# An inverted-bottleneck convolution on one core: expansion of 8x8 patches without their borders, borders copied inside SBUF

## The reference

```python
def _L0_conv_ref(x, ...):                 # 48 channels, windows of 8x8, 4 heads
    h = windows(layernorm(x))
    q, k, v = qkv(h); attn = softmax(q @ k.T * hd**-0.5 + bias[rel_idx])
    xf = shortcut + proj(attn @ v)
    return xf + fc2(gelu(fc1(layernorm(xf))))

def _L1_conv_ref(x, w1, ..., wd, ..., w2, ...):      # 48 -> 288 -> 48 channels
    h = jnp.einsum('oc,bchw->bohw', w1, x)
    h = jax.nn.relu(_bn(h, g1, b1, m1, v1))
    h = conv_general_dilated(h, wd, padding=((1, 1), (1, 1)), feature_group_count=HID)   # 3x3, depthwise
    h = jax.nn.relu(_bn(h, gd, bd, md, vd))
    h = jnp.einsum('oc,bchw->bohw', w2, h)
    return x + _bn(h, g2, b2, m2, v2)
```

## Time and profile before

| | |
|---|---|
| median of 3 runs | 1952.91 us (1952.12 to 1954.72) |
| span of the profiled execution | 1952.0 us |
| TensorE busy (PE / PEld) | 1870.2 us, 96% / 1565.2 us, 80% |
| VectorE busy | 1445.8 us, 74% |
| ScalarE busy | 1322.8 us, 68% |
| GpSimd busy | 647.1 us, 33% |
| HBM read and written | 128.36 and 54.72 MB, 94 GB/s over the span |
| mean granted TensorE clock | 0.993 of full speed |

### The profile page before, as it was taken

The page is one execution under the profiler, slowest core; times in us unless marked ns, Lnnn a source line. Parts: engine busy times, 40 slices in busy tenths (PEclk is TensorE's granted clock), DMA queues, the critical chain, the costliest instruction groups (busy, mean ns, idle before and its releaser), DMA issues.

```text
span 1952.0 us, 74705 instructions
## 1 busy us (share of the span) xinstructions
PE 1870.2 (96%) x29960; PEld 1565.2 (80%) x29960; DVE 1445.8 (74%) x2650; ACT 1322.8 (68%) x2838; POOL 647.1 (33%) x869
## 2 busy tenths in 40 slices
PE   5999999999999996999999999999999999999998
PEld 4888888888888885555555899999999999999997
DVE  5999999999999997666667556566566566566564
ACT  2788878878888885555555666666666666666665
POOL 4333333333333333413100434325334343344240
PEclk9999999999999998999999999999999999999999
DMA  2222222222222222777664444545363454445331
GB/s 67 68 73 76 78 73 76 77 73 76 77 72 77 74 76 77 182 171 179 161 150 111 97 108 126 99 113 126 87 147 86 112 137 102 103 129 105 99 111 34
DMA packets 286410, 198.43 MB, mean 102 GB/s; under 512 B 225991, under 2 KB 275672, under 8 KB 276504
## 3 DMA queue, kind: packets, MB, share of 16 engines
q1 hardware_dynamic: 282114, 189.12, 37.9%
q0 software_dynamic: 2368, 6.25, 1.5%
q10 hardware_dynamic: 1750, 0.39, 0.1%
HBM read 128.36 MB, written 54.72 MB: 94 GB/s over the span
## 4 chain that ended last, share of the span: by engine, by line
PE 56%; ACT 2%; DMA 1%; issue 1%; DVE 0%; SPq 0%; ACTq 0%; DVEq 0%
PE psum L1126 14%; PE psum L1145 13%; PE psum L1171 9%; PE psum L1180 5%; PE psum L680 5%; PE psum L661 3%; PE psum L651 3%; PE psum L666 2%; ACT h2T L1227 1%; DMA room<-tok_mid 1%; ACT h L884 1%; DMA room<-in_ident 0%; ACT room L750 0%; DVE room L885 0%; DVE room L712 0%
## 5 line engine op out<-in xcount | busy, mean ns | idle before, releaser
L934 POOL TENSOR_TENSOR mats<-mats,dscale 112x2048 f32<-112x2048 f32 x72 | 260.8, 3622 | 315.0 <-DMA mats<-in_taps 312.6
L1126 PE MATMUL psum<-ew,xp 64*100 64x96 f32 x6144 | 322.4, 252 | 16.8 <-ACT h L884 13.5
L885 DVE TENSOR_SCALAR h<-psum 100x384 f32<-100x384 f32 x384 | 211.9, 557 | 151.7 <-PE psum L1126 141.6
L1126 PEld LDWEIGHTS psum<-ew,xp 64*100 64x100 f32 x6144 | 295.5, 165 | 26.3 <-ACT h L884 18.6
L1227 ACT ACTIVATE h2T<-psum 96x1024 f32<-96x1024 f32 x192 | 195.6, 1019 | 177.5 <-PE psum L1180 177.5
L1145 PE MATMUL psum<-h,mats 101*64 101x128 f32 x4608 | 269.2, 274 | 1.6 <-issue 0.9
L1145 PEld LDWEIGHTS psum<-h,mats 101*64 101x64 f32 x4608 | 252.0, 137 | 11.8 <-issue 2.0
L884 ACT ACTIVATE room<-psum 64x512 f32<-64x512 f32 (+1 forms) x384 | 206.1, 537 | 78.1 <-PE psum L1145 71.5
L344 PE MATMUL psum<-kb,qa 128*64 128x256 f32 x2048 | 244.0, 380 | 0.8 <-DVE prob L443 0.8
L885 DVE TENSOR_SCALAR room<-psum 64x512 f32<-64x512 f32 (+1 forms) x288 | 174.2, 605 | 64.7 <-PE psum L1145 58.8
L884 ACT ACTIVATE h<-psum 100x384 f32<-100x384 f32 x384 | 186.6, 486 | 48.1 <-PE psum L1126 34.1
(11 more groups left out here) (154 smaller groups left out, 3228.3 us busy)
## 6 DMA issues: line engine op xcount, KB each, us to landing
mats<-in_taps SPq DMA_DIRECT2D x69, 896.0 KB, 5.9
tok_mid<-mid SPq DMA_DIRECT2D x128, 224.0 KB, 1.9
room<-tok_mid SPq DMA_DIRECT2D x64, 448.0 KB, 4.4
piece<-img_mid SPq DMA_DIRECT2D x196, 63.8 KB, 2.4
img_mid<-room SPq DMA_DIRECT2D x128, 97.5 KB, 3.0
kb<-kk SPq DMA_DIRECT2D x512, 24.0 KB
out<-yc SPq DMA_DIRECT2D x32, 384.0 KB, 4.5
scratch<-in_x_tokens SPq DMA_DIRECT2D x126, 96.0 KB, 1.9
```

The costliest lines, as they stand in the source:

```text
L885: return nc.vector.tensor_scalar(dst, src, 0.0, None, ALU.max)
L934: nc.gpsimd.tensor_tensor(m, m, bc(scale[0:MROWS, at:at + TCH], 2, POUT), ALU.mult).then_inc(mats_scaled, 1)
L1126: mm = nc.tensor.matmul(ring[(j + u) % 4][0:PIN, p:4 * CH:4], xp[hx][rows, 2 * j + p, :], w1[rows, c, :], start=True, stop=True)
```

## The change

The border of a patch is no longer expanded with it. `h1` gets another set of lanes: 0 to 63 are the patch's own pixels; TOP (64 to 71), BOTTOM (72 to 79), LEFT (80 to 87) and RIGHT (88 to 95) are the pixels around it, EDGE (96 to 103) one column of pixels of the neighbouring half image, CORNERS (104 to 107) the four corners, and lane 108 holds ones. Patches of a patch column stand 17 apart (GAP), with a column of zeros between them, 137 columns in all (NQ), so that the copy of a neighbour's row is a shift by one column.

- Expansion: two patches at a time (128 columns of weights) straight from the loaded half image, 8 iterations of 8 matmuls; then two short rounds (8 columns of weights) for the edge column. Each bank is evacuated by two instructions of 64 lanes, ACT for u = 0 and DVE for u = 1, and by one of 8 lanes on DVE in the edge rounds.
- Border values: when all of a chunk's expansion has been evacuated, SP issues copies from `h1` to `h1`: top and bottom for each third of the channels, and with the first third the edge column and six rows of corners (nine copies, and three more that bring zeros in the first chunk of a half). POOL issues left and right for each third, on its own queue. TensorE waits for them ahead of depthwise units 0, 2 and 4.
- `mats` holds all 288 channels; it is loaded during the MLP and scaled once, in the first three chunks.
- Turns 0 to 3 stand between the expansion's iterations; then come projections 0 to 3, turns 4 to 7, whose copies ACT and DVE share, and projections 4 to 7. The depthwise part starts behind them, with all six units.
- The half image is loaded in one piece for each u (`load_half`), plus eight loads of single columns (`load_edge`, runs of one number) that the first expansion of a half waits for; SP issues those of the first two halves behind the MLP's last store.
- `img_mid` and `out` are laid out by patch columns; the MLP works in `tail` and the end of `room`; `dynamic_dma_scratch_size` is set to 8192.

The diff, cut to what is added around these points (the cutting and loading of `piece` and `scale_mats` for each chunk go):

```diff
-PIN, POUT = (PH + 2) * (PW + 2), PH * PW
+PIN, POUT = (PH + 2) * (PW + 2) + PH, PH * PW
+GAP = PR + 1
+NQ = PC * GAP + 1
+TOP, BOTTOM, LEFT, RIGHT = POUT, POUT + PW, POUT + 2 * PW, POUT + 3 * PW
+EDGE = POUT + 4 * PW
+CORNERS = EDGE + PH
+ROUNDS = PC + 2
...
+        def evacuate_expand(by_act, k, it, u, part):
+            at = first_of(it // 2 + PC // 2 * u) + PR // 2 * (it % 2) + 4 * part
+            src = ring[(2 * it + u) % 4][POUT * part:POUT * part + POUT, 0:4 * CH]
+            return relu(by_act, h1[0:POUT, :, at:at + 4], src.rearrange("q (c p) -> q c p", p=4))
...
+        def load_edge(eng, h):
+            b, hx = divmod(h, 2)
+            column = d["img_cols"][:, PC - 1 if hx else PC, :]
+            for r in range(2):
+                for t in range(4):
+                    at = H * PW * t + POUT * (4 * b + 2 * r)
+                    src = column[:, at:at + 2 * POUT].rearrange("c (y x) -> c y x", x=PW)[:, :, PW - 1 if hx else 0]
+                    with nc.allow_non_contiguous_dma(reason="one column of pixels"):
+                        eng.dma_start(xp[hx][ONE * r:ONE * r + C, HALF_PIX + 2 * PH * t:HALF_PIX + 2 * PH * (t + 1)], src)\
+                            .then_inc(x_loaded[hx], 16)
+        def halo(eng, put, chs, lanes, at, first, end, shift):
+            count = len(range(P)[lanes])
+            eng.dma_start(h1[at:at + count, chs, first:end], h1[lanes, chs, first + shift:end + shift]).then_inc(put, 16)
+        def expanded(eng, k):
+            eng.wait_ge(unit_act, act_before_expand(k) + ACT_EXPAND)
+            eng.wait_ge(unit_dve, dve_before_expand(k) + DVE_EXPAND)
...
+                expanded(pool, k)
+                for g in range(LOADS):
+                    chs = slice(TCH * g, TCH * (g + 1))
+                    halo(pool, sides_put[g], chs, slice(PW - 1, POUT, PW), LEFT, first_of(1), NQ - 1, -GAP)
+                    halo(pool, sides_put[g], chs, slice(0, POUT, PW), RIGHT, 1, NQ - 1 - GAP, GAP)
...
+            for h in range(2):
+                load_edge(sp, h)
...
+            def halos(k):
+                expanded(sp, k)
+                for g in range(LOADS):
+                    chs = slice(TCH * g, TCH * (g + 1))
+                    halo(sp, halo_put[g], chs, slice(POUT - PW, POUT), TOP, 1, NQ - 1, -1)
+                    halo(sp, halo_put[g], chs, slice(0, PW), BOTTOM, 1, NQ - 1, 1)
+                    if g == 0:
+                        halo(sp, halo_put[0], every, slice(EDGE, EDGE + PH), LEFT if hx else RIGHT, seen, seen + PR, 0)
+                        halo(sp, halo_put[0], every, slice(EDGE + PH - 1, EDGE + PH), CORNERS + 1 - hx, seen, seen + PR, -1)
+                        halo(sp, halo_put[0], every, slice(EDGE, EDGE + 1), CORNERS + 3 - hx, seen, seen + PR, 1)
+                        halo(sp, halo_put[0], every, slice(POUT - 1, POUT), CORNERS, first_of(1), NQ - 1, -GAP - 1)
+                        halo(sp, halo_put[0], every, slice(POUT - PW, POUT - PW + 1), CORNERS + 1, 1, NQ - 1 - GAP, GAP - 1)
+                        halo(sp, halo_put[0], every, slice(PW - 1, PW), CORNERS + 2, first_of(1), NQ - 1, -GAP + 1)
+                        halo(sp, halo_put[0], every, slice(0, 1), CORNERS + 3, 1, NQ - 1 - GAP, GAP + 1)
+                        if c == 0:
...
+            for k in range(CHUNKS_ALL):
+                if k + 1 < CHUNKS_ALL:
+                    halos(k + 1)
+                if c == 0 and 0 < h < HALVES - 1:
+                    load_half(sp, h + 1, x_loaded)
+                    load_edge(sp, h + 1)
+                if c == CHUNKS - 1:
+                    for block in range(BLOCKS):
+                        store(h, block)
...
+            def depthwise(k, d):
+                    pe.wait_ge(halo_put[g], halos_put(k, g))
+                    pe.wait_ge(sides_put[g], 16 * 2 * (k + 1))
...
+                for u in range(DEPTHS):
                     depthwise(k, u)
...
+                    for it in range(ROUNDS):
+                        expand(k + 1, it)
+                        n = turn_behind(it)
+                        if n is not None:
+                            turn(k, n, last)
+                for n in range(BATCH):
+                    project(k, n)
+                for n in range(BATCH, NSTEP):
+                    turn(k, n, last)
+                for n in range(BATCH, NSTEP):
+                    project(k, n)
```

More of the change, by code:

```diff
@@ L1079, in chunk @@
[L1079 to L1090 removed]
+                    sp.dma_start(d["out"][2 * h + r, :, part], y[64 * r:64 * r + C, part]).then_inc(y_stored[block], 16)
@@ new lines, in turn @@
+            def turn(k, n, last):
+                if n == 0:
+                    emptied(k, DEPTHS)
+                before = n - 2 if last or n > BATCH else n - 1
+                if n == BATCH + 1 and not last:
+                    pe.wait_ge(unit_dve, dve_before_expand(k + 1) + DVE_EXPAND - 2)
+                elif before >= 0:
+                    pe.wait_ge(copied, NSTEP * k + before + 1)
+                    if before >= BATCH:
+                        pe.wait_ge(copied_dve, BATCH * k + before - BATCH + 1)
+                pc, a, _ = STEPS[n]
+                for p in range(PART):
+                    for r in range(2):
+                        rows = slice(POUT * r, POUT * r + POUT)
+                        mm = nc.tensor.transpose(turned_at(n, last)[0:CH, r, POUT * p:POUT * p + POUT],
+                                                 h2[rows, PR * pc + a + 4 * (p % 2) + p // 2, :], ident[rows, :])
+                mm.then_inc(turned, 1)
@@ L1230, in first, with copy @@
-            def first():
-                expanded(0, range(0, EXPANDS, 2))
-                for s in range(2):
-                    act.wait_ge(img_stored[s], 32 * (STRIPS // 2))
-            schedule(act, first, chunk)
+            def copy(k, n, last):
+                act.wait_ge(turned, NSTEP * k + n + 1)
+                r = 2 if n < BATCH else 1
+                nc.scalar.activation(h2T[n % TBUFS][0:CH, 0:r, :], turned_at(n, last)[0:CH, 0:r, 0:POUT * PART], ACT.Copy)\
+                    .then_inc(copied, 1)
@@ new lines, in _ @@
+            for it in range(ROUNDS):
+                empty_expand(0, it)
+            for s in range(2):
+                act.wait_ge(img_stored[s], 32 * (STRIPS // 2))
+            for k in range(CHUNKS_ALL):
+                last = k == CHUNKS_ALL - 1
+                filtered(k)
+                if last:
+                    for n in range(BATCH):
+                        copy(k, n, last)
+                else:
+                    for it in range(ROUNDS):
+                        empty_expand(k + 1, it)
+                        n = turn_behind(it)
+                        if n is not None:
+                            copy(k, n, last)
+                for n in range(BATCH, NSTEP):
+                    copy(k, n, last)
```

518 lines of the change are left out of this document (220 added, 298 removed).

## The result

The changed kernel takes **2450.4 us** (2448.5 to 2453.8), against 1953.6 before: 1.254 times as long, 95% interval 1.253 to 1.256. The forecast was 2056, and its range ended at 2310. The profiled execution has a span of 2446.7 us, 494.7 more than before.

A forecast was written before the change was run, and what follows sets the result against it. TensorE was taken to bound the kernel, busy 34.99 of 35.98 us a chunk. Span 1952.0 - 37 (chunk work) + 111 (copy waits) + 29 (start) = 2055, 2056 with 0.9 for the median; range 1925 to 2310.

The forecast's parts named there:

- phases without waits: One chunk's expansion 13.4, projections and turns 10.0, depthwise 11.0 us: 34.4 against 36.0, minus 1.6 us a chunk.
- the wait: TensorE ahead of depthwise: copies 11.9 us against 8.75 of cover; 3.6 us in 16 chunks, 7.6 in 7.
- Top and bottom: First two SyncE border copies, 138 KB each: 1.9 us apiece by bytes, 1.1 by runs; the larger taken.
- The corners: Four long corner copies of 45 KB in SyncE's queue: 0.62 us each by bytes.
- kb's rate: Existing SBUF copy kb<-kk, 24 KB into 12 lanes in 0.40 us: 4.2 ns a run, 73 GB/s.
- The short runs: SyncE's border-column copy, 768 runs of 64 bytes, 3.2 us; two short corners, 0.40 us each.
- GpSimd's six copies: Copies on GpSimd's own queue: land within SyncE's nine; lengthen the wait if transfer engines are shared; not in the sum.
- That the copies wait on SyncE's issue rather than on bytes: Sign at the wait ahead of depthwise: if issue limits the copies instead of bytes, the prediction falls.
- The second, few lanes: Border copies: rate belongs to lanes, 6.1 GB/s each; first third lands at 18.7 us; 2300 us; chance 0.25.
- The first rival, hidden copies: Ahead of depthwise unit 0: issue limits, ordinary chunks wait for nothing, half beginnings 1.2 us; 1945 us; chance 0.37.
- The third rival, half speed for unit 0 after a wait: Depthwise unit 0: waits lower the clock, 1.8 us a chunk, 40 us more; range only, no chance given.
- The start: First expansion 13 us later, uncovered first copies 14, low clock 2: 29 us together.

The follow-up runs named there:

- free copies: The changed kernel without any border copy and without the waits for them: 2000.5 us.
- the best that still makes every copy: The changed kernel with the lanes that the copies write placed four apart, same copies, bytes and queues: 2340.9 us.
- the two fillings: The changed kernel with needless matmuls on TensorE ahead of the wait for the copies: 128 narrow ones, 2461.1 us; 28 of 512 columns, 2442.8 us.

## Why the prediction was wrong

**The sum, part by part.** Forecast against measured, per chunk and for 23 of them: phases without waits 34.4 against 36.8 (55 us), the wait 4.8 on average against 16.4 (266 us), the clock nothing against 1.8 (41 us); and the first depthwise instruction at 1146.9 instead of the forecast's 1114.5 (32 us). Together 394 us, by which the forecast missed.

**The wait: the step that failed.** Of the 11.9 us, which are 18.2 without GpSimd's copies, two terms were mis-sized, and one was left out of the sum. (1) Top and bottom, 2 x 1.9 taken: 5.5 measured. (2) The corners, 4 x 0.62 by kb's rate and 0.2 to land: 8.3. The short runs, 3.2 + 0.8, were high by 1.0 and the start right. The forecast took 73 GB/s, seen on 12 lanes in a burst of 0.40 us, for a rate that lasts. The corners' packets start at that rate (68 GB/s), but until TensorE starts the lanes have taken 22 GB/s (181 KB in 8.3 us); the burst of 24 KB didn't show the difference. (3) GpSimd's six copies were put "in the range, not in the sum", as if another queue were another path: they cost 6.3 us a chunk (16.4 against 10.1 without them), the largest single term. The prediction's condition was "where they share transfer engines", and the packets show that they do.

**SyncE's issue.** That the copies wait on SyncE's issue rather than on bytes was named as a sign against the prediction, and in part it came. The chain of the changed kernel that ended last, by engine as a share of the span:

```profile
PE 27%; SPq 17%; ACT 11%; DMA 10%; DVE 2%; issue 1%; ACTq 0%; DVEq 0%
```

Without GpSimd's copies, the issues of the edge column and the two short corners behind it took 2.3, 3.1 and 1.6 us, and the first long corner was issued at 1179.71, 8.6 us behind the first copy. In the 3.0 us between the bottom's last packet and the corners' first the transfer engines were only 0.14 busy, so up to 3.0 of the 18.2 us may be issue. With GpSimd's copies beside them the first two of these issues took 3.7 and 6.5 us. Whether the queue held SyncE up or the short runs are slow to issue stays open.

**The rivals.** The second, few lanes, had the right mechanism for the corners: its 18.7 us for the first third stands beside 18.2 measured without GpSimd's copies, and its 7.4 and 0.2 for the corners beside 8.3. Its way to 2300 was still not this run's: further thirds didn't wait, GpSimd's copies weren't in it, and its top and bottom (2 x 2.8 against 5.5) came out right although spreading the lanes written didn't speed the first ones up. The prediction's sign for this rival, a wait over 9 us, came too, but of the 16.4 GpSimd's copies made 6.3. The Trainium skill's port rule (page "SBUF — State Buffer", section "Door 1: The DMA port swizzle") agrees with the corners, 22 GB/s to the landing where it has some 27 a port, and with a top copy as far as the eight neighbouring lanes read go: two ports, and 44 to 45 GB/s measured, twice the corners' rate. The 73 GB/s of the later copies onto spread lanes don't speak against it, since top and bottom read different lanes and may overlap there. No run changed the lanes that top and bottom read, so this stays argued. The first rival, hidden copies at 1945, would not have come out even with free copies: that is 2000.

**The phases without waits.** TensorE got back less than claimed: the pairs with 128 columns take 0.137 us (the group below: 193.4 us over 22 chunks of 64 pairs), not 0.112, so 8.8 + 1.7 instead of 8.6 us, a gain of 1.5 where the forecast had 3.4.

```profile
L1086 PE MATMUL psum<-ew,xp 64*128 64x96 f32 x2816 | 193.4, 279 | 34.0 <-ACT h L837 33.1 <-DVE h L838 0.8
L837 ACT ACTIVATE h<-psum 64x384 f32<-64x384 f32 x352 | 190.7, 542 | 21.3 <-PE psum L1086 14.3
L1195 ACT ACTIVATE tail<-psum 96x1024 f32<-96x1024 f32 x88 | 89.8, 1020 | 2.1
```

Here the row of L374 in the earlier trace rows, 0.128, was nearer than the value chosen between it and 0.094. That the expansion runs at ScalarE's pace was right; the sum counted three turned copies of 0.95, and four of 1.02 fall into it: 13.4 became 14.4. "The depthwise part is unchanged" was wrong by 0.8 us: before, unit 0 ran ahead of the last projections, which covered its evacuation; behind them, unit 2 waits for it.

**The clock.** The third rival, half speed for unit 0 after a wait, was right in kind and size: 1.8 us a chunk. It had been kept out of the sum because no row of a chunk showed it; the earlier trace rows did, after an idle stretch of the same kernel.

**The start.** 13 us were forecast for the later expansion, and 31 came (1104.1 against 1073.2): the columns cost 10, and the MLP, which was priced at nothing, ended 22 us later, 5 by the memsets beside VectorE and 14 by two loads of half images ahead of its strips (2 to 3 us are not accounted for). From the first expansion to the first depthwise instruction it was 42.8 us instead of the forecast's 28.1: there TensorE waits 29.2 us for the same copies, with nothing to cover them.

**What held.** The place of the wait and its releaser, the wait's greater length where a half begins (17.1 against 16.0), ScalarE's pace, and the sign.

## What to carry to other kernels

Price a copy by what its landing costs over the whole burst, not by the rate of a short one, and add up all copies of a stage, on whatever queue they are issued, against the cover: here some 25 us of copies stood against 9 us of cover, and no order or shape that was tried brought them under it (the best that still makes every copy took 2341 us). Ask also what remains if the new cost were nothing: with 2000 us against 1953 this kernel would not have won even with free copies, since TensorE's freed time was taken up again by other engines on the path and by the start.

## What the hardware showed that was not expected

- Two queues of copies inside SBUF take turns packet by packet: GpSimd's nine-run packets (1.6 us) held SyncE's one-run packets (0.03 us) down to six a us, without a shared lane.
- Into four neighbouring lanes 22 GB/s arrive, counted until TensorE starts, though packets start at 68; lanes four apart shorten the four corners from 8.3 to 5.2 us.
- SyncE's issue of a copy isn't a fixed 0.6 to 0.85 us: behind 768 short runs one took up to 7.1 us.
- In a wait of 16 us the clock fell to the lower level (0.50), and the first two depthwise units after it ran at 0.54 to 0.70 on average. Behind the shorter idle stretches of the two fillings it came out either way: 0.68 behind 2.3 us in one chunk, 1.00 behind 3.6 us in another.
- A top copy moved at 44 GB/s onto neighbouring and 45 onto spread lanes, at a DMA share of 0.35, and at 45 in eight long runs. So neither the lanes written nor the length of the runs limits it; whether the lanes read do, or the engines used, was not settled. Behind each of these copies the trace has 8 packets of 4 bytes, behind each corner 16; the Trainium skill, page "DMA: Bandwidth & Descriptors", section "Why a DMA increments its semaphore by 16 and not by 1", has one such packet for each engine used, and an engine count that divides the slowest dimension, here eight lanes. The trace agrees with eight engines for a copy over eight lanes; a top copy over sixteen wasn't tried.
